# A one-core decoder layer: attention, cross-attention and quantised feed-forward stages rewritten, nine unread TensorE products at the start, feed-forward blocks of four token tiles in place of two

## The reference, cut to what matters

```python
def _layernorm(x, axis=-1, eps=1e-05):
    m = jnp.mean(x, axis=axis, keepdims=True)
    v = jnp.var(x, axis=axis, keepdims=True)
    return (x - m) / jnp.sqrt(v + eps)
# attention: x is (16, 64, 256), H = 16 heads of D = 16
    q = proj(Wq, bq); k = proj(Wk, bk); v = proj(Wv, bv)
    scores = jnp.einsum('bhqd,bhkd->bhqk', q, k) / math.sqrt(D)
    scores = jnp.where(causal[None, None], -jnp.inf, scores)
    scores = scores + _alibi_bias(S)[None]
    probs = jax.nn.softmax(scores, axis=-1)
    out = jnp.einsum('bhqk,bhkd->bhqd', probs, v)
    return out.transpose(0, 2, 1, 3).reshape(B, S, E) @ Wo.T + bo
# cross-attention, one head, 64 memory tokens with a mask per sequence
    scores = jnp.einsum('bsd,bmd->bsm', hidden_states, memory_tokens) * scale
    scores = jnp.where(memory_mask[:, None, :], scores, neg_inf)
    readout = jnp.einsum('bsm,bmd->bsd', jax.nn.softmax(scores, axis=-1), memory_tokens)
    out = jnp.where(valid_b[:, None, None], readout, jnp.zeros_like(readout))
# feed-forward, 256 -> 1024 -> 256, weights rounded to 4-bit codes with a scale per block of 32 rows
    h = jax.nn.gelu(inputs @ quantised(up_kernel) + up_bias)
    y = h @ quantised(down_kernel) + down_bias
# the layer
    x = x + attention(_layernorm(x))
    x = x + cross_attention(_layernorm(x), ctx, mask)
    x = x + feed_forward(_layernorm(x))
```

## Time and profile before

| | |
|---|---|
| median of 3 runs | 159.94 us |
| the 3 runs | 157.60, 159.94, 162.42 us |
| span of the profiled execution | 157.1 us |
| PE busy | 127.9 us (81%) |
| DVE busy | 126.1 us (80%) |
| ACT busy | 96.4 us (61%) |
| POOL busy | 54.1 us (34%) |
| mean granted TensorE clock | 0.967 |

### The profile page before, as it was taken

The page is one execution under the profiler, slowest core; times in us unless marked ns, Lnnn a source line. Parts: engine busy times, 40 slices in busy tenths (PEclk is TensorE's granted clock), DMA queues, the critical chain, the costliest instruction groups (busy, mean ns, idle before and its releaser), DMA issues. The chain is left out here.

```text
span 157.1 us, 2931 instructions
## 1 busy us (share of the span) xinstructions
PE 127.9 (81%) x878; PEld 87.3 (56%) x878; DVE 126.1 (80%) x345; ACT 96.4 (61%) x212; POOL 54.1 (34%) x92
## 2 busy tenths in 40 slices
PE   0149999987992497991977999898999999979992
PEld 0027444312471174550565657677788989759991
DVE  1854998799999999779899988796785789697551
ACT  3014559996936045582322742666989899899970
POOL 8969920052211240310403343732540254052000
PEclk9999999999999789998579999999999999999999
DMA  4999993000020341910000000000000000020011
GB/s 95 321 329 341 368 274 144 2 2 4 2 67 0 87 180 30 280 30 0 0 0 4 0 0 0 4 2 0 4 0 2 4 33 31 3 73 0 0 67 67
DMA packets 9135, 11.20 MB, mean 71 GB/s; under 512 B 1665, under 2 KB 7937, under 8 KB 8993
## 3 DMA queue, kind: packets, MB, share of 16 engines
q1 hardware_dynamic: 7776, 9.90, 20.3%
q10 hardware_dynamic: 1344, 1.13, 2.2%
HBM read 9.45 MB, written 1.05 MB: 67 GB/s over the span
## 5 line engine op out<-in xcount | busy, mean ns | idle before, releaser
L556 POOL TENSOR_TENSOR s_sb<-s_sb,s_max 128x512 f32<-128x512 f32 x16 | 17.3, 1084 | 50.1 <-DVE s_max L828 50.1
L969 PE MATMUL bank<-k,q_T 128*64 128x512 f32 x64 | 20.0, 681 | 5.2 <-DVE s_sb L825 5.2
L1064 PE MATMUL bank<-xn_T,w_T 128*128 128x256 f16 x128 | 19.2, 273 | 1.2 <-ACT h_sb L688 0.7
L1080 PE MATMUL bank<-w_down_q,h_hi 128*128 128x256 f32 x64 | 18.7, 318 | 0.0
L636 ACT ACTIVATE p_T<-bank 128x512 f32<-128x512 f32 x16 | 9.6, 599 | 13.1 <-PE bank L990 10.3
L932 PE MATMUL bank<-const,xn 128*128 128x128 f32 x48 | 10.3, 304 | 8.8 <-DVE xn L785 8.7
L990 PEld LDWEIGHTS bank<-v,p_T 128*64 128x64 f32 x256 | 14.1, 148 | 5.9 <-issue 4.7
L902 DVE TENSOR_TENSOR h_lo<-h_sb,h_hi 128x256 fp32r<-128x256 f32 x32 | 13.4, 437 | 4.8 <-ACT h_sb L688 4.8
L528 POOL TENSOR_SCALAR var_eps<-mean_var 128x1 f32<-128x1 f32 x24 | 5.8, 240 | 31.7 <-DVE mean_var L777 31.6
L688 ACT ACTIVATE h_hi<-bank,bias_cols 128x256 fp32r<-128x256 f32 x32 | 15.3, 478 | 2.3 <-PE bank L1080 0.7
L990 PE MATMUL bank<-v,p_T 128*64 128x34 f32 x256 | 15.7, 235 | 1.2 <-ACT q_T L643 1.1
(11 more groups left out here) (82 smaller groups left out, 271.6 us busy)
## 6 DMA issues: line engine op xcount, KB each, us to landing
raw<-in_W_up_T_dram SPq DMA_DIRECT2D x1, 1024.0 KB, 10.5
ctx_T<-in_ctx_by_feature_dram SPq DMA_DIRECT2D x1, 1024.0 KB, 9.7
ctx_sb<-in_ctx_dram SPq DMA_DIRECT2D x1, 1024.0 KB, 9.9
raw<-in_W_up_dram SPq DMA_DIRECT2D x1, 1024.0 KB, 4.9
raw<-in_W_down_T_dram SPq DMA_DIRECT2D x1, 1024.0 KB, 4.8
raw<-in_W_down_dram SPq DMA_DIRECT2D x1, 1024.0 KB, 6.6
out_dram<-x_sb SPq DMA_DIRECT2D x8, 128.0 KB, 1.7
x_sb<-in_x_dram SPq DMA_DIRECT2D x4, 128.0 KB, 3.1
```

Of the source, the lines that this page charges most:

```text
L556: pool.tensor_tensor(tile, tile, s_max[:, u % S_RING, :].unsqueeze(2).broadcast_to([P, HC, S]), ALU.subtract).then_inc(centred, 1)
L969: last = pe.matmul(dst[b * S:(b + 1) * S, :].rearrange("p (h k) -> p h k", h=HC), q_T[:, c, tok], k2[:, c, :, tok], start=True, stop=True)
L1064: last = pe.matmul(dst[:, 0:GN], w_up_q[:, c, f * P:(f + 1) * P], xn_T16[:, g * GT:(g + 1) * GT, at16:at16 + P], start=(k == 0), stop=(k = ...
L1080: last = pe.matmul(dst, src[:, i % H_RING, t * P:(t + 1) * P], w_down_q[:, f, :], start=(f == 0 and part == 0 and t == 0), stop=(f == FC - ...
```

## The change

Nearly every stage is written anew. In the order of the data:

- **Start.** POOL fills a tile `warm`, and PE multiplies it nine times (128x512) into bank 7, seven times before the first turn and once behind each of the first two. Nothing reads the products. The bias table is loaded before the second half of `x`.
- **Norms.** LN2 and LN3 are normalised on POOL, with one more small POOL step (`shift`); LN1 stays on DVE.
- **k and v.** `k2` has four slots for 128 features instead of eight: 16 products of 128x512, four of them on DVE, five on ACT, seven on POOL. A slot holds one head in each half of 64 partitions, and the weights' rows are laid out for that on the host. `v` is computed into the right partitions by twice as many products of 128 columns and 64 output rows, so its DMAs and the spreading on ACT are gone.
- **Scores.** PE puts the bias table into the banks itself (`s_bias`, one product of 512 columns for each unit; it is kept in two rounded parts, made by `bias_hi` and `bias_lo`), and then adds the scores of a whole tile in eight products of 256 columns with 64 input rows and 64 output rows. DVE takes the maximum and subtracts, both straight from the bank. POOL has no part in it. The bias of `v` is folded into the output bias once (`bo_fold`, `bo_sum`). Both units of a tile are turned back and copied together.
- **Cross-attention.** A PE product adds the mask; ACT exponentiates from the bank; DVE's masking step and the second scale step are gone.
- **Quantisation** runs over whole matrices, 128x2048 at a time, in 10 and 11 instructions. `w_down_q` is bf16, and a power of two scales the hidden values (`h_scale`, six small DVE steps).
- **Feed-forward** in two groups of four tiles, 16 blocks in place of 32: four `up` products of 512 columns, one gelu on ACT, a rounded fp16 half on ACT (first group) or POOL (second group), the rest on DVE, and eight `down` products of 256 columns. Each group has two banks.
- The table of costs and weights behind `schedule()` is new, so that all queues have a new order.

The core of the diff:

```diff
-GT = 2
-GROUPS = TILES // GT
-GN = GT * P
-GELU_RING = 4
-H_RING = 5
+GROUPS = ((0, 1, 2, 3), (4, 5, 6, 7))
+DOWN_BANKS = ((2, 3), (4, 5))
+BLOCKS = [(g, f) for g in range(len(GROUPS)) for f in range(FC)]
+GN = HALF * P
+H_RING = 4
+WARM = 9
...
+K_ENGINE = {(0, 0): ("act", "act", "dve", "dve"), (0, 1): ("act", "pool", "dve", "dve"),
+            (1, 0): ("pool", "pool", "pool", "act"), (1, 1): ("pool", "pool", "pool", "act")}
+HI_ENGINE = ["act" if i < FC else "pool" for i in range(len(BLOCKS))]
...
+                if stage == "norm" and at[0] != LN1:
+                    n, t = at
+                    ring = XN_RING[n]
+                    if t >= len(ring):
+                        pool.wait_ge(xn_turned[n], t - len(ring) + 1)
+                    pool.tensor_scalar(xn[:, ring[t % len(ring)], :], x_sb[:, t, :], rstd[:, n, t:t + 1],
+                                       shift[:, n, t:t + 1], ALU.mult, ALU.add).then_inc(xn_ready[n], 1)
...
-                if stage == "centre":
-                    u, = at
-                    pool.wait_ge(max_ready, u + 1)
-                    tile = s_sb[:, u % S_RING, :].rearrange("p (h k) -> p h k", h=HC)
-                    pool.tensor_tensor(tile, tile, s_max[:, u % S_RING, :].unsqueeze(2).broadcast_to([P, HC, S]),
-                                       ALU.subtract).then_inc(centred, 1)
...
+                if stage == "s_max":
                     u, = at
+                    dve.tensor_reduce(s_max[:, u, :], bank[u % EC][:, :].rearrange("p (h k) -> p h k", h=HU), AX_X,
+                                      ALU.max).then_inc(max_ready, 1)
+                if stage == "s_sub":
+                    u, = at
...
-                    dve.tensor_tensor(steps_tile, bank[u % 2][:, :], alibi_sb[:, u % EC, :],
-                                      ALU.add).then_inc(scores_added, 1)
-                    dve.wait_ge(scores_added, u + 1)
-                    dve.tensor_reduce(s_max[:, u % S_RING, :], steps_tile.rearrange("p (h k) -> p h k", h=HC), AX_X,
-                                      ALU.max).then_inc(max_ready, 1)
+                    dve.tensor_tensor(s_sb[:, u % S_RING, :].rearrange("p (h k) -> p h k", h=HU),
+                                      bank[u % EC][:, :].rearrange("p (h k) -> p h k", h=HU),
+                                      s_max[:, u, :].unsqueeze(2).broadcast_to([P, HU, S]),
+                                      ALU.subtract).then_inc(subtracted, 1)
...
+                if stage == "warm":
+                    pe.wait_ge(warm_filled, 1)
+                    pe.matmul(claim(7)[:, :], warm[:, 0:P], warm[:, :], start=True, stop=True)
...
-                    for j in range(2):
+                    done = 2 * h + pair + 1
+                    dst = claim(v_bank(h, pair), (v_even_ready, done), (v_odd_ready, done))
+                    for j in range(4):
+                        t, b = HALF * h + 2 * pair + j // 2, j % 2
                         for i in range(EC):
-                            last = pe.matmul(dst[:, j * E:(j + 1) * E],
-                                             xn_T[:, HALF * h + 2 * pair + j, i * P:(i + 1) * P], w_T[:, WV, i, :],
-                                             start=(i == 0), stop=(i == EC - 1))
+                            for odd in range(2):
+                                last = pe.matmul(dst[odd * S:(odd + 1) * S, j * P:(j + 1) * P],
+                                                 xn_T[:, t, i * P + b * S:i * P + (b + 1) * S],
+                                                 w_T[:, WV, i, odd * P:(odd + 1) * P],
+                                                 start=(i == 0), stop=(i == EC - 1), skip_group_check=True)
+                if stage == "s_bias":
+                    t, r = at
+                    pe.wait_ge(twin_ready, 1)
+                    pe.wait_ge(s_bias_lo, 1)
+                    dst = claim(r, (subtracted, EC * t + r + 1))
+                    pe.matmul(dst[:, :], twin[:, :], s_bias[:, r * HU * S:(r + 1) * HU * S], start=True, stop=False,
+                              skip_group_check=True)
                 if stage == "scores":
-                    u, = at
-                    t, c = divmod(u, EC)
+                    t, = at
                     h = t // HALF
-                    pe.wait_ge(q_copied, EC * h + c + 1)
-                    for copied, value in keys_copied(h, c):
-                        pe.wait_ge(copied, value)
-                    dst = claim(u % 2, (scores_added, u + 1))
-                    for b in range(2):
-                        tok = slice(t * P + b * S, t * P + (b + 1) * S)
-                        last = pe.matmul(dst[b * S:(b + 1) * S, :].rearrange("p (h k) -> p h k", h=HC), q_T[:, c, tok],
-                                         k2[:, c, :, tok], start=True, stop=True)
+                    pe.wait_ge(q_copied, EC * (h + 1))
+                    for c in range(EC):
+                        for copied, value in keys_copied(h, c):
+                            pe.wait_ge(copied, value)
+                    for c in range(EC):
+                        for r in range(EC):
+                            for b in range(2):
+                                tok = slice(t * P + b * S, t * P + (b + 1) * S)
+                                part = slice(r * S, (r + 1) * S)
+                                last = pe.matmul(
+                                    bank[r][b * S:(b + 1) * S, c * SLOTS * S:(c + 1) * SLOTS * S].rearrange(
+                                        "p (h k) -> p h k", h=SLOTS),
+                                    q_T[part, c, tok], k2[part, c, :, tok], start=False, stop=(c == EC - 1),
+                                    skip_group_check=True)
                     last.then_inc(scores_ready, 1)
...
-                            last = pe.matmul(dst[:, 0:GN], w_up_q[:, c, f * P:(f + 1) * P],
-                                             xn_T16[:, g * GT:(g + 1) * GT, at16:at16 + P],
+                            last = pe.matmul(dst[:, 0:block_columns(i)], w_up_q[:, c, f * P:(f + 1) * P],
+                                             xn_T16[:, tiles[0]:tiles[-1] + 1, at16:at16 + P],
                                              start=(k == 0), stop=(k == 3))
                             k += 1
                     last.then_inc(up_ready, 1)
...
-                        claim(2 + g % 2, (final_ready, GT * (g + 1)))
-                    for t in range(GT):
-                        dst = bank[2 + g % 2][:, t * E:(t + 1) * E]
+                        for j, b in enumerate(DOWN_BANKS[g]):
+                            claim(b, (final_ready, GROUPS[g][2 * j + 1] + 1))
+                    for j, t in enumerate(GROUPS[g]):
+                        dst = bank[DOWN_BANKS[g][j // 2]][:, j % 2 * E:(j % 2 + 1) * E]
                         for part, src in enumerate((h_hi, h_lo)):
-                            last = pe.matmul(dst, src[:, i % H_RING, t * P:(t + 1) * P], w_down_q[:, f, :],
-                                             start=(f == 0 and part == 0 and t == 0),
+                            last = pe.matmul(dst, src[:, i % H_RING, j * P:(j + 1) * P], w_down_q[:, f, :],
```

850 lines of the change are left out of this document (471 added, 379 removed).

## The result

The changed kernel takes 146.12 us (median of four runs, 145.73 to 146.60); the kernel before took 160.97 us beside it. The ratio is 0.9205 (95% interval 0.908 to 0.933): faster by about 8%. The forecast was 139.8 us, a ratio of 0.874. The time lies inside the range of 132 to 147, but near its upper end: by the ratio, set against the 159.94 us from which the forecast started, it would be 147.2, just past it. In a later session the changed kernel took 146.00 us, at 0.9151 (0.911 to 0.919) of the kernel before.

A forecast was written before the change was run, and what follows sets the result against it. PE and DVE were taken as the bound, together 1.73 us of work per us: start to 32.8, middle 75.4 to 108.2, rest to 133.2, end 3.8, span 137.0, plus 2.8: 139.8 us, ratio 0.874; 8 in 10 for 132 to 147.

The forecast's parts named there:

- With the unread products ahead I take full speed.: Start, up to the first maximum: PE at full speed, folded bias 0.96 and `v` 1.89 us; first scores end at 32.8.
- the start stays cold: 141.7: Rival: unread products leave PE idle again before `v`; 1.9 us more, 141.7 us; inside the forecast range given 0.70.
- q and k then start at 11.11 + ...: Start, PE: `W_vo_T` loaded at 11.11, then folded bias 0.96, `v` 1.89 and turns 0.4, so q and k at 14.4.
- It fits as it fitted before: Start, DVE: its early list, 21.6 us before, becomes 23.0 us and is done by the first scores.
- The middle: First maximum to first `down` product: DVE 63.9 plus PE 66.5 us, 130.4 in all, takes 75.4 us, ending at 108.2.
- the pairs (1.8): Rival for a tile's scores: only pairs of products overlap, 1.8 us not 0.9; total 143.4 us; inside the range given 0.70.
- At 1.73 us of work per us: Middle: PE and DVE together get 1.73 us of work done per us, as in the kernel before.
- the length of one tile's chain, with both below 80%: Sign of error: the middle is bound by one tile's chain instead of PE and DVE, both busy below 80%.
- POOL and DVE block each other: Rival: POOL steps cost DVE up to 11.6 us, total 146.5, likelier 142; lock or serial scores up to 157: 0.09.
- The rest: From the first `down` product to PE's end: 24.0 us of PE work plus 1.0 for gaps, ending at 133.2.
- if the last piece waited for gelu or POOL: Sign of error: behind the first `down` product PE waits, instead of running without gaps for 25 us.
- The rival on the slow side: PE falls to half speed between tiles; 23 us of 66.5 at it gives 163, half of it 172; slower: 0.02.

The follow-up runs named there:

- Experiment 2: Changed kernel with 31 unread products in place of nine, drawn out up to the folded bias: 144.18 us, ratio 0.909 to the kernel before.
- Experiment 1: Changed kernel without its nine unread products, all else in the same order: 146.04 us, ratio 0.920 to the kernel before.
- experiment 6: Changed kernel with 31 unread products and ScalarE's queue issuing `W_vo_T` ahead of `W_qk_T`: 143.17 us, ratio 0.889 to the kernel before.
- experiment 4: Changed kernel with POOL's norm as one `subtract, mult` step, without the shift: 149.47 us, ratio 0.940 to the kernel before.
- experiment 7: Changed kernel with six of eleven steps quantising the down weights cut to 64 columns, so weights not the reference's: 142.99 us, ratio 0.883 to the kernel before.
- experiment 8: Changed kernel with 31 unread products, `W_vo_T` issued first, second and third norms on DVE without the shift: 141.53 us, ratio 0.8875 to the kernel before.
- experiment 9: Changed kernel with 31 unread products, `W_vo_T` issued first, eleven more unread products at the middle's end: 143.19 us, ratio 0.8965 to the kernel before.
- experiment 11: Changed kernel with the feed-forward in four groups of two tiles, one bank each, order planned anew: 148.41 us, ratio 0.919 to the kernel before.

## Why the prediction was wrong, step by step

**The start failed: "With the unread products ahead I take full speed."** 37.75 against 32.8. I had counted the products and not looked at when they end: seven of 0.45 us from 1.46 leave 3.78 us without work ahead of the first turn, and the earlier trace rows showed already what PE does after an idle time. The folded bias, `v` and their turns were priced at 3.3 us (0.96 + 1.89 + 0.4) and took 6.0 (12.28 to 18.27): 2.7 of the 4.9 us missed. Experiment 2 shows that this is the clock: with products up to the folded bias the same stretch takes 3.1 (12.72 to 15.80). Experiment 1 shows no gain by the nine. I had priced this case, "the start stays cold: 141.7", at 1.9, which leaves out that the folded bias is slow as well, and had put it inside the forecast's range instead of giving it the place of the likelier case.

**"q and k then start at 11.11 + ...": the moment at which the work on `W_vo_T` begins was taken from the kernel before.** It came 1.2 us later, at 12.28. The folded bias and `v` stand ahead of q and k in PE's queue and both need `W_vo_T`, the second of two transfers in ScalarE's queue. But the load is only the last 0.46 us. Ahead of the folded bias stands a turn that waits for a DVE norm until 11.16, and that norm is one of two that took 2.15 us beside a POOL memset of 1.91:

```profile
9.18 2.15 DVE L850 TENSOR_SCALAR xn<-x_sb,mean_var,rstd 128x256 f32<-128x256 f32 x2 [0.60 <-PE bank L1007]
```

```profile
8.96 1.91 POOL L606 MEMSET v<- 128x2176 f32 x1
```

The prediction had named this ("POOL's memsets can hold up DVE") and given it no price. Asking for `W_vo_T` first changes the load alone, and of three profiles that have it one has a folded bias well ahead of experiment 2's, one a little and one not (experiment 6).

**"It fits as it fitted before": DVE's early list was late.** From the first of q and k to the first scores the sum had 17.5 us (14.4 to 31.9); it took 18.3 (18.27 to 36.59). DVE had 25.05 us to do in the start and not 23.0, and at 31.04 PE waits 0.71 us for its copy of `v`; the same wait stands in experiments 2 and 6, which also take 18.3. The three terms, 2.7, 1.2 and 0.8, and 0.2 from the scores to their first maximum, make the 4.9. In experiment 6 q and k began 0.6 before the forecast's 14.4, and this 0.8 made up for it: that its start ends near 32.8 is partly luck too.

**The middle was right in size: 76.7 against 75.4**, and so were its sums. DVE 64.2 against 63.9, PE 69.2 against 66.5, shares of 1.74 against 1.73. PE's single terms were less so: the `v2` products of a unit, priced at 0.85, take 0.59 from start to start (4 us less in all), and what makes up for it is in part the low clock from 100 to 107 (0.85 us in the first four `up` products alone). Outside the middle DVE had 3.7 us more than forecast, so 105.3 in all and not 101.3. Scores of a tile: 1.02 against 0.9, all four quarters of the array together, so the pairs (1.8) and no overlap (3.6) are out, and whatever the scores cost beyond that is 0.12 us a tile. The Trainium skill, "TensorEngine Tiling (Array Packing)", Tiling Modes, states that a change of tiling mode drains TensorE. No row isolates that: a drain behind the scores would lie within the 0.12 us, one ahead of them in the distance of the product before, which is 0.23 us for a bias product of 512 columns (40.97 to 41.20 in the chain). DVE's wide steps, from its groups in the changed kernel:

```profile
L808 DVE TENSOR_SCALAR q_x<-q_code 128x2048 bf16<-128x2048 bf16 x2 | 1.4, 688 | 0.0
...
L797 DVE TENSOR_TENSOR q_x<-q_x,q_code 128x2048 bf16<-128x2048 bf16 x2 | 2.4, 1209 | 0.0
```

0.69 and 1.21, forecast 0.75 and 1.25.

**But the reason given for it holds only in part.** "At 1.73 us of work per us" treats the piece as bound by two engines, and I named as a sign of error "the length of one tile's chain, with both below 80%". From 80 to 114.42 that is so: PE is busy 79% and DVE 80%, which add up to 1.58, and from 88 to 101.5 the chain runs through POOL, var_eps, `rstd`, shift and norm of one tile after the other:

```profile
96.22 0.55 POOL var_eps L583
96.77 0.07 issue
96.84 0.57 POOL rstd L587
97.50 1.35 POOL shift L591
98.86 0.10 issue
98.95 0.55 POOL xn L601
```

Experiments 4, 7 and 8 agree: 6.7 us more on POOL made the middle 1.9 longer, 4.75 us less on DVE (and 3.2 less on POOL) made it 1.9 shorter, and moving the norms from POOL to DVE gave 1.3. In the first 42 us of the middle PE is busy 42.13 of 42.25 us (window from 37.75 to 80), and the shares add up to 1.87. So 1.73 holds in neither part; the mean of 1.87 and 1.58, by their lengths, happens to be 1.74. That the sum came out right is luck.

**POOL and DVE block each other: true, and it is POOL that loses.** The shift above takes 1.34 us where others take 0.27, and ends with a DVE step of two inputs that started 0.1 us later:

```profile
97.50 1.34 POOL L591 TENSOR_SCALAR shift<-mean_var,rstd 128x1 f32<-128x1 f32 x1
```

```profile
97.60 1.19 DVE L797 TENSOR_TENSOR q_x<-q_x,q_code 128x2048 bf16<-128x2048 bf16 x1
```

POOL waits for DVE here, and its small steps suffer most. The Trainium skill, "SBUF — State Buffer", Who interferes with whom, has this: a DVE step with two inputs in SBUF and a GpSimd step that reads SBUF hold each other up, and so does a DVE step in a two-port mode. The trace agrees with the first of these. In the start two DVE norms took 2.15 us beside a POOL memset, after two that took 0.70; by that rule it would be the second, but no row shows DVE's mode. The same section of the Trainium skill gives the ports to the one that issues first, and there the trace doesn't agree: by the records POOL's step began first and was the one that waited. I had priced the blocking as DVE's loss, up to 11.6 us; DVE's sum in the middle is 0.3 us above the forecast. POOL's 16 shifts take 392 ns in the mean, its shortest 267, and experiment 7 shows about 1.0 us of this kind on the path.

**The rest was right in size (25.4 against 25.0), but "PE without gaps" was not.** PE is busy 23.58 of 25.38 us, and the last norm's turn waits for POOL:

```profile
120.22 0.41 PE L1007 MATMUL bank<-const,xn 128*128 128x128 f32 x2 [1.70 <-POOL xn L601]
```

The chain lies on POOL from 108.26 to 120.22, and only from there on PE; gelu was not late. The forecast had 1.0 us for gaps, for another reason. So this sign of error, "if the last piece waited for gelu or POOL", came as well. The end was right (4.0 against 3.8).

**The rival on the slow side didn't come.** PE never fell to the low clock between tiles while the middle was full; it did from about 100 to 107, where filling it gained nothing (experiment 9). The rival's price for half of the work at the low clock should be 173 by its own sum (139.8 + 33.3), not 172.

What stays open: what decides in an execution whether `v` reaches full speed, what the swapped transfers give by themselves, and how much of the time under the combined limit of POOL and DVE could be had by another order of the last 15 us; no order but the planner's was tried with experiment 8's engines.

## What to carry to other kernels

Look at whether unread products run at full speed themselves, and at the idle time between their last one and the first product that matters. If they last up to that product, see that they don't become what it waits for. Before a late start is put down to a load, look at how much of it is a wait for the load, and compare several executions: the same start, swap and unread products gave first scores at 32.1, 33.5 and 34.1. A sum of shares can size a piece well while another engine's chain is on the path; read the chain, and test with one load taken away on each engine, and look at whether the others' loads stayed as they were.

## What the runs showed of the hardware that was not expected

- POOL's `tensor_scalar` on 128x256 with two operands per row takes 625 ns as `mult, add` and 1437 ns as `subtract, mult` (experiment 4); DVE takes 501 to 582 ns for the latter.
- POOL's `h_hi` of 256 columns took 0.71 us in experiment 11, as long as 512 columns (0.69): half of it lies under a DVE step of two inputs.

```profile
126.53 0.71 POOL L641 TENSOR_SCALAR h_hi<-h_sb,h_factor 128x256 f16<-128x256 f32 x1 [0.16 <-ACT h_sb L756]
```

```profile
126.40 0.48 DVE L973 SCALAR_TENSOR_TENSOR h_lo<-h_sb,h_factor,h_hi 128x256 f16<-128x256 f32 x1 [0.38 <-POOL h_hi L641]
```

- The granted clock in the records can read 1.00 where products take twice their time (experiment 1, 7 to 20 us: folded bias 2.07 us for 1.03 in experiment 2), and the same kernel gave `v` in 3.63 us in one execution and 2.79 in another.
- Sixteen products of 64x64 with 256 columns take 1.02 us, the time of four of 128x64 with 512 (0.9) and a little.
